# Split the routed down weights once during the attention, and keep four experts in the ring instead of six

## What is computed

```python
h = embed(x)                                # hot rows gathered, cold rows projected from 128 values
h = h + attention(layernorm(h))             # 2 x 1024 tokens, 16 heads of 32, causal
xt = layernorm(h)
probs = softmax(xt @ Wr.T + bias)           # 16 experts
w, idx = top_k(probs, 2); w = w / (sum(w) + 1e-9)
g, u = xt @ Wg[e], xt @ Wu[e]               # 512 -> 256, e in idx
y = (silu(g) * u) @ Wd[e]                   # 256 -> 512
h = h + sum_k w_k * y_k + (silu(xt @ sWg) * (xt @ sWu)) @ sWd
```

## Time and profile before

| | us |
|---|---|
| median of 3 runs | 969.42 (968.51 to 969.42) |
| the profiled execution, its own time | 968.75 |
| its span, first to last instruction | 966.9 |
| attention, from the first scores to the last heads | about 110 to 567 |
| output projection, router, shared expert | about 567 to 715 |
| routed tiles | about 715 to 957 |
| last adds and the end | 957 to 967 |

### The profile page before, as it was taken

The page is one execution under the profiler, slowest core; times in us unless marked ns, Lnnn a source line. Parts: engine busy times, 40 slices in busy tenths (PEclk is TensorE's granted clock), DMA queues, the critical chain, the costliest instruction groups (busy, mean ns, idle before and its releaser), DMA issues.

```text
span 966.9 us, 21709 instructions
## 1 busy us (share of the span) xinstructions
PE 902.7 (93%) x6859; PEld 683.4 (71%) x6859; DVE 657.3 (68%) x1653; ACT 599.2 (62%) x1314; POOL 444.8 (46%) x494
## 2 busy tenths in 40 slices
PE   6779799999999999999997999999999999999995
PEld 5335578787887978878785677667766766676673
DVE  8895567576666757666675767768876666666662
ACT  6322487776768777777877833231156777777772
POOL 9377554533525346251500416633355476357332
PEclk9699899999999999999999999999999999999998
DMA  6135442323414143332313521261559478737430
GB/s 231 42 100 141 122 118 52 95 64 86 113 51 102 49 113 75 78 96 54 97 44 101 206 94 71 83 277 55 185 177 382 138 138 188 256 62 129 61 43 0
DMA packets 60513, 110.52 MB, mean 114 GB/s; under 512 B 15412, under 2 KB 21556, under 8 KB 58098
## 3 DMA queue, kind: packets, MB, share of 16 engines
q1 hardware_dynamic: 48082, 87.15, 29.1%
q0 software_dynamic: 12320, 21.99, 11.8%
HBM read 53.03 MB, written 25.17 MB: 81 GB/s over the span
## 4 chain that ended last, share of the span: by engine, by line
PE 76%; DVE 9%; issue 6%; SPq 4%; ACT 3%; POOL 1%; DMA 0%; DVEq 0%; POOLq 0%; ACTq 0%
PE psum L1563 13%; PE psum L692 11%; PE psum L1641 8%; PE psum L705 6%; PE psum L635 6%; PE psum L682 6%; PE psum L648 5%; PE psum L657 4%; SPq L450 4%; PE psum L1482 3%; PE psum L1595 2%; PE psum L1585 2%; PE psum L708 1%; DVE psum L821 1%; PE psum L1574 1%
## 5 line engine op out<-in xcount | busy, mean ns | idle before, releaser
L779 ACT ACTIVATE probs<-psum,nmax 128x128 f32<-128x128 f32 (+7 forms) x256 | 191.3, 747 | 37.4 <-DVE nmax L821 35.1
L821 DVE CUSTOM_DVE_ANT_0 psum<-psum,mask_row 128x128 f32<-128x128 f32 (+7 forms) x256 | 192.2, 767 | 27.6 <-PE psum L682 26.4
L692 PE MATMUL psum<-ident,probs 128*128 128x128 f32 x1152 | 175.2, 276 | 12.5 <-ACT probs L779 5.6
L692 PEld LDWEIGHTS psum<-ident,probs 128*128 128x128 f32 x1152 | 134.4, 140 | 48.3 <-ACT probs L779 18.0
L764 ACT COPY probsT<-psum 128x512 f32<-128x512 f32 (+3 forms) x256 | 129.2, 505 | 33.1 <-PE psum L692 30.7
L1055 POOL DMA_INDIRECT out<-xnT,slot_out x47 | 80.0, 1703 | 102.6 <-DMA out<-xnT,slot_out 73.7
L487 POOL CAST part_hi<-full 128x512 fp32r<-128x512 f32 x28 | 17.1, 610 | 206.6 <-ACT full L552 160.8
L682 PE MATMUL psum<-k_low,q_stack 128*128 128x512 f32 (+2 forms) x256 | 105.1, 418 | 5.2 <-ACT probs L779 2.6
L836 DVE TENSOR_TENSOR attnT<-psum,z_rows 128x128 f32<-128x128 f32 x64 | 18.7, 292 | 111.6 <-ACT z_rows L786 111.6
L1641 PE MATMUL psum<-w_dn,gated_T 128*128 x188 | 88.6, 593 | 1.0 <-ACT gated_T L1118 1.0
L1405 DVE TENSOR_TENSOR w_lo<-w_gu,w_hi 128x1024 fp32r<-128x1024 f32 x48 | 58.7, 1225 | 39.1 <-ACT w_hi L1147 37.7
(11 more groups left out here) (278 smaller groups left out, 2118.8 us busy)
## 6 DMA issues: line engine op xcount, KB each, us to landing
w_gu<-in_wgu SPq DMA_DIRECT2D x16, 1024.0 KB, 6.8
q_stack<-part_hi SPq DMA_DIRECT2D x128, 64.0 KB, 2.0
q_stack<-part_lo SPq DMA_DIRECT2D x128, 64.0 KB, 2.0
w_dn<-in_wd SPq DMA_DIRECT2D x16, 512.0 KB, 9.3
out<-acc SPq DMA_DIRECT2D x17, 256.0 KB, 3.9
hot_all<-xn SPq DMA_DIRECT2D x4, 1024.0 KB, 8.3
h_scratch<-hot_all SPq DMA_DIRECT2D x16, 256.0 KB
k_low<-part_hi SPq DMA_DIRECT2D x64, 64.0 KB, 2.0
```

Source lines behind the costliest of these rows:

```text
L692: mm = pe.transpose(bank(4 + m % 2)[:, (j - 4 * k) * P:(j - 4 * k + 1) * P], probs[n % PSLOTS][:, j * P:(j + 1) * P], ident[:, :])
L779: act.activation(probs[n % PSLOTS][:, 0:(i + 1) * P], score_bank(n)[:, 0:(i + 1) * P], ACT.Exp, bias=nmax[:, n % 4:n % 4 + 1], scale=-1.0, ...
L821: dve.tensor_tensor_reduce(out=row, in0=row, in1=mask_row[:, (QT - 1 - i) * P:QT * P], scale=1.0, scalar=3.0e38, op0=ALU.add, op1=ALU.min, ...
```

## The change

All 16 experts' down weights are loaded once during the attention (0.5 MB each, SP), split by POOL into a high and a low part, and stored to a DRAM scratch of 1 MB an expert (POOL's DMA queue). Two sets of buffers in SBUF, each for one expert at a time, serve for it; they lie where `attnT` of the head groups 2 and 3 is written later, so DVE waits for the stores before it writes those. In the routed stage the ring has four slots; an expert's load is now `w_gu` (1 MB) and the two parts of the down weights (1 MB). The parts' slots lie on `acc`, four tiles each, so the first four experts' parts are loaded as those tiles have been stored. The down product becomes six fp32r matmuls; ACT makes the high part of the gated values (the copy it made before, with another type), DVE the low part. `weight_high(j + 2, 0)` now stands ahead of `y_scale(j - 1)`. The rows' buffers are no longer on `acc`, so 14 gathers are issued ahead of the wait for the stored output instead of 8.

```diff
-WRING = 6
-EARLY_EXPERTS = 4
+WRING = 4
...
+DN_BOTH = 14
+DN_FIRST = {1: (0, 1), 2: (4, 5), 3: (8, 9), 4: (12, 13), 5: (15,)}
+DN_SECOND = {1: (2, 3), 2: (6, 7), 3: (10, 11), 4: (14,)}
...
+        dn_dram = nc.dram_tensor("dn_scratch", [E, P, 4 * D], F32, kind="Internal").ap()
...
+        def dn_set(e):
+            return (e % 2, e // 2) if e < DN_BOTH else (1, DN_BOTH // 2 + e - DN_BOTH)
+
+        def load_down(sp, e):
+            s, n = dn_set(e)
+            if n:
+                sp.wait_ge(s_dnst[s], 16 * (n + 1))
+            sp.dma_start(dn_part[:, s, 1, :].bitcast(F32), a["wd"][e].rearrange("p k n -> p (k n)")
+                         ).then_inc(s_dnraw[s], 16)
+
+        def split_down(pool, e):
+            s, n = dn_set(e)
+            pool.wait_ge(s_dnraw[s], 16 * (n + 1))
+            passed(pool)
+            raw = dn_part[:, s, 1, :].bitcast(F32)
+            pool.tensor_copy(dn_part[:, s, 0, :], raw).then_inc(s_dnsp, 1)
+            pool.wait_ge(s_dnsp, 2 * e + 1)
+            pool.tensor_tensor(dn_part[:, s, 1, :], raw, dn_part[:, s, 0, :].bitcast(F32),
+                               ALU.subtract).then_inc(s_dnsp, 1)
+            pool.wait_ge(s_dnsp, 2 * e + 2)
+            passed(pool)
+            pool.dma_start(dn_dram[e], dn_part[:, s, :, :].rearrange("p a n -> p (a n)").bitcast(F32)
+                           ).then_inc(s_dnst[s], 16)
...
@@ att_sp, for each unit u @@
                     load_wq(sp, u // 2 + 1)
+                for e in DN_FIRST.get(u, ()):
+                    load_down(sp, e)
                 sp.wait_ge(s_S, HEAD + (u - 1) * STEPS + NARROW)
                 for side in range(2):
                     stack_half(sp, u, side, 0)
+                for e in DN_SECOND.get(u, ()):
+                    load_down(sp, e)
...
@@ att_pool, for each unit u @@
+                for e in DN_SECOND.get(u - 1, ()):
+                    split_down(pool, e)
                 split_part(pool, u, 0, 0)
                 for c in range(KC):
                     split_rows_in(pool, u, 1, c)
                 split_part(pool, u, 1, 0)
                 split_part(pool, u, 0, 1)
+                early, late = (DN_FIRST.get(u, ()) + (None, None))[0:2]
+                if early is not None:
+                    split_down(pool, early)
                 split_part(pool, u, 1, 1)
+                if late is not None:
+                    split_down(pool, late)
...
@@ moe_sp @@
+            for e in range(WRING):
+                load_gate_up(e)
+            for e in range(WRING):
+                sp.wait_ge(s_wl[e], 16)
+                sp.sem_inc(s_wr, 1)
...
             for c in range(NT):
                 store(c)
...
+                if c == NT - 1:
+                    sp.dma_start(out[T:T + P, :], acc[:, NT - 1, :]).then_inc(s_pad, 16)
+                    sp.wait_ge(s_pad, 16)
+                if c % (NT // WRING) == NT // WRING - 1:
                     sp.wait_ge(s_out, 16 * (c + 1))
+                    load_down_parts(c // (NT // WRING))
             sp.wait_ge(s_plan, PLANNED)
             for e in range(WRING, E):
                 done = sp.value_load(tiles_to_i[0:1, e - WRING:e - WRING + 1], min_val=0, max_val=TILES)
                 sp.wait_ge(s_y, done + SHARED)
-                load(e)
+                load_gate_up(e)
+                load_down_parts(e)
                 if e > WRING:
                     ready(e - 1)
...
@@ moe_act, routed tiles @@
                 if j >= 1:
-                    turn_copy(SHARED + j - 1, (j - 1) % 2)
+                    turn_high(SHARED + j - 1)
                 weight_high(j + 1, 1)
                 silu(SHARED + j, j % 2)
                 row_high(j + 2)
+                weight_high(j + 2, 0)
                 if j >= 1:
                     y_scale(j - 1)
-                weight_high(j + 2, 0)
...
@@ moe_dve, routed tiles @@
+                if j >= 1:
+                    turn_low(SHARED + j - 1)
                 weight_low(j + 1, 1)
...
@@ down_of @@
                 for k in range(2):
-                    mm = pe.matmul(bank(6 + p), gated_T[:, p, k * P:(k + 1) * P],
-                                   w_dn[:, bass.ds(half, 1), k, :].rearrange("p o n -> p (o n)"), start=(k == 0),
-                                   stop=(k == 1))
+                    for t, (g, part) in enumerate(((gs_hi, 0), (gs_lo, 0), (gs_hi, 2))):
+                        mm = pe.matmul(bank(6 + p), g[:, p, k * P:(k + 1) * P],
+                                       w_dn[:, bass.ds(half, 1), part + k, :].rearrange("p o n -> p (o n)"),
+                                       start=(k == 0 and t == 0), stop=(k == 1 and t == 2))
```

More of the change, by code:

```diff
@@ L161, in build @@
         ring_ctx.close()
+        spare_ctx = ExitStack()
+        sb("first_heads_room", [P, 2 * T], F32, spare_ctx)
+        dn_part = sb("dn_part", [P, 2, 2, 2 * D], F32R, spare_ctx)
+        spare_ctx.close()
         attnT = sb("attnT", [P, GROUPS * T])
@@ L187, in build @@
         att_ctx.close()
+        ring_ctx = ExitStack()
+        w_dn = sb("w_dn", [P, WRING, 4, D], F32R, ring_ctx)
+        ring_ctx.close()
         acc = sb("acc", [P, NT, D])
@@ L200, in build @@
         half_cols = lambda i, side: xnT[:, i // 2, side * SEQ + (i % 2) * D:side * SEQ + (i % 2) * D + D]
-        x_rows = [half_cols(i, 0) for i in range(X_RING // 2)] + [acc[:, i, :] for i in range(X_RING // 2, NT)]
         y_rows = [half_cols(i, 1) for i in range(ROUTED_RING)]
@@ L221, in build @@
         ws_lo = sb("ws_lo", [P, KC + 2, D], F32R)
-        w_dn = sb("w_dn", [P, WRING, 2, D])
-        ws_full = w_dn[:, :, :, :].rearrange("p s k n -> p (s k) n")
+        x_more = sb("x_more", [P, X_RING // 2, D])
+        sb("rows_room", [P, 4, D])
+        ws_full = x_more
+        x_rows = [half_cols(i, 0) for i in range(X_RING // 2)] + [x_more[:, i, :] for i in range(X_RING // 2)]
         xs_hi = sb("xs_hi", [P, 2, D], F32R)
@@ L321, in build @@
         s_wl = [sem(f"expert_loaded{i}") for i in range(WRING)]
+        s_dnraw = [sem(f"down_weights_loaded{i}") for i in range(2)]
+        s_dnsp = sem("down_weights_split")
         s_wr = sem("expert_weights_ready")
@@ L834, in normalize @@
                 dve.wait_ge(s_ZR, HEAD + u * QT + i + 1)
+                if b == 0 and i == 0 and g == 2:
+                    dve.wait_ge(s_dnst[0], 16 * (DN_BOTH // 2 + 1))
+                if b == 0 and i == 0 and g == 3:
+                    dve.wait_ge(s_dnst[1], 16 * (E - DN_BOTH // 2 + 1))
                 dst = attnT[:, g * T + b * SEQ + i * P:g * T + b * SEQ + (i + 1) * P]
@@ L919, in moe_sp, with load_gate_up, load_down_parts @@
                 sp.dma_start(xn2_dram[c * P:(c + 1) * P, :], xn2[:, c % 2, :]).then_inc(s_xst[c % 2], 16)
-            def load(e):
+            def load_gate_up(e):
+                sp.dma_start(w_gu[:, e % WRING, :, :], a["wgu"][e]).then_inc(s_wl[e % WRING], 16)
+            def load_down_parts(e):
                 s = e % WRING
-                sp.dma_start(w_gu[:, s, :, :], a["wgu"][e]).then_inc(s_wl[s], 16)
-                sp.dma_start(w_dn[:, s, :, :], a["wd"][e]).then_inc(s_wl[s], 16)
+                sp.dma_start(w_dn[:, s, :, :].rearrange("p k n -> p (k n)").bitcast(F32), dn_dram[e]
+                             ).then_inc(s_wl[s], 16)
             def ready(e):
@@ L939, in moe_sp @@
             sp.wait_ge(s_wslo, NT)
-            for e in range(EARLY_EXPERTS):
-                load(e)
-            for e in range(EARLY_EXPERTS):
-                ready(e)
+            for e in range(WRING):
[3 more added lines that the diff above has]
+                sp.sem_inc(s_wr, 1)
+            for s in range(2):
+                sp.wait_ge(s_dnst[s], 16 * (DN_BOTH // 2 + s * (E - DN_BOTH) + 1))
             for c in range(NT):
                 store(c)
-                if c == NT // 2:
+                if c == NT - 1:
+                    sp.dma_start(out[T:T + P, :], acc[:, NT - 1, :]).then_inc(s_pad, 16)
+                    sp.wait_ge(s_pad, 16)
+                if c % (NT // WRING) == NT // WRING - 1:
                     sp.wait_ge(s_out, 16 * (c + 1))
[L948 to L953, removed]
+                    load_down_parts(c // (NT // WRING))
             sp.wait_ge(s_plan, PLANNED)
@@ L1058, in add @@
                     compute_op=ALU.add).then_inc(s_yadd[j % 2], 16)
-            for j in range(X_RING // 2):
+            pool.wait_ge(s_wslo, NT)
+            passed(pool)
+            for j in range(GATHER_AHEAD):
                 gather(j)
@@ L1635, in down_of @@
                 pe.wait_ge(s_gC, SHARED + j + 1)
+                if j < WRING:
+                    pe.wait_ge(s_wl[j], 32)
                 if j < 2:
```

16 lines of the change are left out of this document (4 added, 12 removed).

## The result

The changed kernel took **997.68 us** (median of 4 runs, 993.67 to 999.92) beside 969.08 us before (968.51 to 969.42) on the same chip: ratio **1.0287**, interval 1.0253 to 1.0321, slower. On a second chip, later: 993.35 us beside 967.99, ratio 1.0270 (1.0251 to 1.0288). The forecast was 985 us, 957 to 1003. The profiled run took 993.67 us, 24.9 over that of before; its span was 991.9, 25.0 over.

A forecast was written before the change was run, and what follows sets the result against it. PE was taken to bound the kernel, busy 93% of the span. The terms -15.0 + 16.8 + 10.2 + 2 + 0.8 + 1 + 1 = +16.8 on 968.75 us gave 985 us, range 957 to 1003.

The forecast's parts named there:

- The down product: Routed stage: 47 products go from 1.72 to 1.40 us, -15.0 us, with a period of 4.84 us a tile.
- the term priced at nothing (DVE's low part): Hand-over to the down product: DVE's low part adds 0.42 us, hidden, cost nothing; at most 20 us without cover.
- The ring: Routed stage, four slots: single-tile experts lose 16.8 and 10.2 us; extras +2 (expert 3's parts), +0.8 (expert 9).
- L: Routed stage: time from an expert load's issue to its being declared, 10.4 us, bounds 8.0 to 12.6.
- c: Routed stage: time from an expert's declaration to the end of the down product, 4.4 us including 0.5 for hand-overs.
- The stacks: Attention: 1 MB stores beside the upper stacks slow them, 0 to 1 us in six units; +1, bounds 0 to +6.
- POOL's splits: Attention: 61 us of split work over five units, hidden by POOL's waits; cost 0, or 61 with no cover.
- The wait for the first pair's stores: Attention, SP's queue: a unit's second pair waits for these stores, ending near 212 us with 7 us spare.
- The clock: Routed stage: of five new gaps, one slows a down product at half clock; +1 us, bounds 0 and +7.
- the loads did not come sooner: Rival 1, routed stage, chance 0.18: expert loads come sooner, L about 6.5 us, giving 963, or 954 with the ring hidden.
- the steady tiles did gain: Rival 2, routed stage, chance 0.07, claimed the opposite: late gs_lo keeps the period at 5.16 us, giving 1000.
- the third: Rival 3, attention, chance 0.07: stores or SP's waiting hold PE by 3 us or more a unit, giving 1003.

The follow-up runs named there:

- The routed part alone: Changed kernel without the attention's loads, splits and stores, the down parts read from the gate-up tensor instead (output not the reference's): 987.92 us, ratio 1.0201.
- the routed part left out: Kernel before, with the attention's loads, splits and stores of the down weights added and their result not used: 976.98 us, ratio 1.0098.
- The kernel kept busy: Changed kernel with extra matmuls of constants into the free bank ahead of five late down products: 996.44 us, ratio 1.0274.

## Why the prediction was right, and where its sizes were off

**Direction and mechanism were right.** The forecast case came, 12.7 us above its number by the first median (8.4 by the second) and inside its range.

- *The down product, -15.0 us*: right. 1.40 us and a period of 4.84 (968.56 - 891.10 over 16 tiles); nothing spilt over in the steady tiles, as the term priced at nothing (DVE's low part) said.
- *The ring, +29.8 with its extras*: right in kind, 3.7 too low. From the end of tile 0 to that of tile 4 took 33.2 us against 31.6, from tile 18 to 25 52.8 against 50.7. L was forecast at 10.4 and measured 10.7, 10.4, 10.3, 8.7 and 9.8, on average 10.0. The step that failed is **c, 4.4 us, which measured 6.2, 5.8, 6.2, 6.0 and 5.0**, and within it the down product. The path up to the product took 3.23 us each time, where the sum had 3.0: DVE makes the low weights ahead of gs_lo (1.00 us in the chain) where I had put ACT's y_scale (0.69), but ACT's high part of the gated values (0.37) runs beside it, so the error nearly cancels; that is luck. The product was put in at 1.40. Behind a wait it takes 1.66 even at the full clock, and four of the five ran at the low clock for most of it, 2.56 to 2.94. The routed part alone measured +19.5 against a forecast of +15.8 for those terms.
- *The stacks, +1 with a bound of +6*: **mis-sized, the larger miss**, and outside its bound. With the routed part left out, the attention cost +8.6; k_high of unit 2, which was to stay near 245 us, was first taken at 249.8. I had bounded it by the landing of the last key stack alone; what slipped was what SP issues ahead of it: three of unit 2's four groups of query stacks took 0.4 to 2.9 us longer. The second piece, the wait for probsT, no step of mine had: I costed POOL's splits at nothing because POOL had idle time, and did not ask what DVE does while POOL works. The wait for the first pair's stores, which I had looked for in its place, didn't come: SP issued the second loads at 215.15 and stood free until the upper stacks at 222.46.
- *The clock, +1 with a bound of +7*: I took one slow product of five. Against 1.40 the five lost 1.54, 1.16, 1.54, 1.42 and 0.35, together 6.0 us; 0.26 of each is the wait's and not the clock's, which leaves 4.7. That is inside the c above, and the forecast had it apart. The kernel kept busy was not faster, so how much of these 4.7 us the whole time holds isn't shown. The Trainium skill (TensorE: Matmul & The Clock Gate, section HAM oscillation) says that each such gap for DMA makes the clock fall; the trace agrees with the fall in four of the five (0.66, then 0.50 at 744 us, that is 1.2 GHz); the product behind the gap of 3.45 us took 1.75 us, and on the second chip one behind 3.03 us took 1.65.
- *The rivals*: the loads did not come sooner (L), the steady tiles did gain, and PE's wait for the last key stack never reached the 3 us a unit of the third, though its place was the right one (2.9 in the worst unit). The rule of the Trainium skill on which the first leant (DMA: Bandwidth & Descriptors, section Anatomy of one DMA; 6.8 us for an expert's 2.1 MB) is given there for DMAs that GpSimd issues; for SyncE's two loads here it does not agree with the 8.7 to 10.7 us measured, where gathers, adds and a second expert's load share the engines.

## What to carry to other kernels

Count what stands in one declaration: a slot that is handed over only when the last of its tensors was used holds all of them back, and here releasing and declaring them apart was worth 23 to 26 us where the bytes, the ring and the products stayed. When ring depth falls, follow the in-order queues from the declaration to the instruction that frees the next slot, every queued instruction of every engine on the way; the sum of that row sets the period, and only once it is short does bandwidth. An instruction put in to fill a wait has to end before the wait does, or it becomes a cost of its own. Work put on an idle engine isn't free: ask what its stores meet in the transfer queues and what its reads and writes hold up on its neighbour, and measure the addition by itself before the rest is built on it.

## What the runs showed of the hardware

- **GpSimd holds VectorE's copy.** VectorE's 128x128 copy into z_inv takes 0.23 us (median). In the changed kernel one took 1.48. In order of time (start, us):

```profile
285.91 2.35 POOL L487 TENSOR_TENSOR dn_part<-dn_part 128x1024 fp32r<-128x1024 f32 x1
286.87 1.48 DVE L881 COPY z_inv<-z_rec 128x128 f32<-128x128 f32 x1
```

The copy ended at 288.35, just after the subtraction (288.26). Before, where GpSimd's longest subtraction was 1.28 us, the longest such copy was 0.88; after, 1.52. These copies took 24.2 us for 56 instead of 19.8 for 57, and the copies to probsT stand behind them. The Trainium skill (SBUF — State Buffer, section SBUF: two separate sides) says that the two engines share a pair of ports, held for a whole instruction. The trace agrees: the copy ends with the subtraction.

- **Stores from GpSimd's queue slow SyncE's issues.** Four issues of 64 KB took 2.4 to 2.5 us, and 2.9 to 5.4 beside 1 MB stores. An eighth of the bytes brought the landing back from 3.5 to 2.6 us.
- **The products behind five gaps of 2.71 to 5.26 us** took 1.75 to 2.94 us instead of 1.40, with the granted clock at 0.50 behind the first (744 to 746 us) and the third (843 to 847). Keeping PE busy kept the clock at 1.00; the time stayed the same, in a run where one fill cost some 2.5 us itself.
- **The changed kernel's runs scatter** by 6.3 us over four, against 0.9 over the four of the kernel before beside them; on the second chip by 5.2 over five, against 4.5 over seventeen. On the first chip the longest run has the lowest mean clock (999.92 us, 0.965) and the shortest the highest (993.67, 0.976); on the second it is not so (996.11 at 0.975, 990.89 at 0.972). In the kernel kept busy the mean clock was 0.978 to 0.982 in all five runs, and they still lay 5.1 us apart, so the clock alone doesn't make the scatter. What does isn't shown.
